# Two of four column groups of a graph-convolution product by Strassen's scheme

## The reference

```
h   = relu(layernorm(x))                 # x: 8 x 2048 x 128, float32
HW  = h @ W                              # W: 128 x 128
A   = relu((adj + adj.T) / 2)            # 2048 x 2048
D   = sum(A, axis=1);  d = D ** -0.5
L   = I - d[:, None] * A * d[None, :]
out = x + relu(L @ HW)                   # for each of the 8 batches
```

## Time and profile before

| what | value |
|---|---|
| time, median of 3 runs | 430.36 us (428.66 to 430.53) |
| the profiled execution | 428.56 us, its span 426.8 us |
| busy: PE, DVE, ACT, POOL | 394.8, 192.5, 115.0, 181.1 us |
| mean granted TensorE clock | 0.991 |
| matmuls of 512 columns in the main phase | 1536 by the code |
| DMA | 42.39 MB, mean 99 GB/s |

### The profile page before, as it was taken

How to read it: one execution, slowest core, us unless ns; L and a number is a source line. 1 busy time by engine, 2 the same in 40 slices (tenths; PEclk the granted TensorE clock), 3 DMA queues, 4 the chain that set the end, 5 groups by cost and what they waited for, 6 DMA issues and landing times.

```text
span 426.8 us, 5828 instructions
## 1 busy us (share of the span) xinstructions
PE 394.8 (93%) x2193; PEld 208.4 (49%) x2193; DVE 192.5 (45%) x519; ACT 115.0 (27%) x235; POOL 181.1 (42%) x295
## 2 busy tenths in 40 slices
PE   4648678999999999999999999999999999999994
PEld 3548653444444444454545454545454545454541
DVE  2697999979789844144614142431010202010211
ACT  1565986665657420102120102110100001010100
POOL 0088702077599957264955445813020111212211
PEclk9987999999999999999999999999999999999999
DMA  8999995103203343030022020031102020203011
GB/s 271 354 372 384 387 281 152 48 0 96 78 2 111 94 117 98 2 92 9 25 75 74 26 74 25 2 98 42 58 27 73 26 74 26 74 10 90 27 49 49
DMA packets 59820, 42.39 MB, mean 99 GB/s; under 512 B 2320, under 2 KB 51600, under 8 KB 59792
## 3 DMA queue, kind: packets, MB, share of 16 engines
q1 hardware_dynamic: 59792, 42.02, 31.8%
HBM read 33.62 MB, written 8.39 MB: 98 GB/s over the span
## 4 chain that ended last, share of the span: by engine, by line
PE 50%; issue 30%; POOL 7%; SPq 4%; DMA 3%; DVE 2%; ACT 2%; POOLq 0%
PE ps L572 14%; PE ps L573 14%; PE ps L574 14%; POOL sums L286 4%; DMA S<-in_adj_dram 3%; SPq L180 3%; PE ps L522 3%; PE ps L536 2%; POOL dsv L277 1%; SPq L195 1%; ACT S L316 1%; PE ps L586 1%; PE ps L587 1%; PE ps L588 1%; POOL xn L268 1%
## 5 line engine op out<-in xcount | busy, mean ns | idle before, releaser
L573 PE MATMUL ps<-S,hbuf 128*128 128x512 f16 x512 | 194.0, 379 | 0.0
L572 PE MATMUL ps<-S,hbuf 128*128 128x512 f16 x496 | 188.0, 379 | 0.0
L574 PE MATMUL ps<-S,hbuf 128*128 128x512 f16 x496 | 188.0, 379 | 0.0
L286 POOL TENSOR_TENSOR sums<-res,sums 128x512 f32<-128x512 f32 x32 | 42.8, 1343 | 160.9 <-DVE res L420 160.9
L573 PEld LDWEIGHTS ps<-S,hbuf 128*128 128x128 f16 x512 | 50.1, 98 | 56.5
L574 PEld LDWEIGHTS ps<-S,hbuf 128*128 128x128 f16 x496 | 48.5, 98 | 58.5
L572 PEld LDWEIGHTS ps<-S,hbuf 128*128 128x128 f16 x496 | 48.5, 98 | 54.9
L412 DVE SCALAR_TENSOR_TENSOR g<-ps,g 128x512 f16<-128x512 f32 x32 | 21.6, 686 | 114.5 <-ACT g L342 114.5
L342 ACT ACTIVATE g<-ps 128x512 f16<-128x512 f32 x32 | 19.0, 593 | 192.0 <-PE ps L574 191.5
L420 DVE SCALAR_TENSOR_TENSOR res<-ps,dsv 128x512 f32<-128x512 f32 x32 | 22.1, 689 | 75.8 <-PE ps L588 75.8
L336 ACT ACTIVATE S<-S,dneg 128x512 f16<-128x512 f32 x62 | 43.5, 719 | 21.6 <-DVE S L407 19.6
(11 more groups left out here) (69 smaller groups left out, 285.0 us busy)
## 6 DMA issues: line engine op xcount, KB each, us to landing
S<-in_adj_dram SPq DMA_DIRECT2D x16, 1024.0 KB, 12.4
hbuf<-in_x_dram SPq DMA_DIRECT2D x64, 128.0 KB, 3.5
sums<-in_x_dram SPq DMA_DIRECT2D x32, 256.0 KB, 2.8
out_dram<-sums SPq DMA_DIRECT2D x32, 256.0 KB, 2.6
res<-in_L_gnn_W_dram SPq DMA_DIRECT2D x1, 64.0 KB, 1.8
```

The costliest lines, as they stand in the source:

```text
L286: nc.gpsimd.tensor_tensor(sums[:, e % SUMS, :], res[:, e % 2, :], sums[:, e % SUMS, :], ALU.add).then_inc(sum_ready, 1)
L572: nc.tensor.matmul(acc, h_hi, l_hi(t), start=(mt == 0), stop=False)
L573: nc.tensor.matmul(acc, h_hi, l_lo(t), start=False, stop=False)
L574: last = nc.tensor.matmul(acc, h_lo, l_hi(t), start=False, stop=(mt == T - 1))
```

## The change

Groups 0 and 1 are computed as before, now as 8 stages of the four quarters (128 slots). Groups 2 and 3 are computed as one 2 x 2 block product for each quarter: A is the two batches by the two halves of the contraction, B the two halves of the contraction by the two column groups. Instead of eight half products there are seven parts P1 to P7 (Winograd's form of Strassen's scheme), in the order P1, P2, P6, P3, P5, P7, P4, each of 8 steps by 3 matmuls of 512 columns. They are four quarters by seven parts after the 128 slots.

- **Operands of B.** Four forms T1 to T4 are sums of blocks of L. For each of 8 rows of blocks, from slot 33 on every 10 slots, ACT scales one block, DVE makes four forms, ACT and DVE split them. T3 stays in S. The other three are written by ACT's own transfers to a DRAM array `t_forms` (48 transfers of 128 KB) and read back by SP to where L's groups 0 and 1 were, after their last use (6 MB each way).
- **Operands of A.** S1 to S4 are made of the halves of h: `join_pair` on POOL (1024 columns), `combine_pair` on DVE (four instructions of 256 columns), `split_pair_hi` on ACT and `split_pair_lo` on DVE (two instructions of 512 columns each), four pairs to a quarter.
- **Results.** P1 is copied out of PSUM by ACT; seven sums on DVE for each quarter give the four tiles, which then go through the same steps as every tile.
- **Normalisation.** With two groups to a quarter in the plain stages, quarter 1 is due at slot 32, quarter 2 at 64, quarter 3 at 96. The power on POOL gives way to a square root on ACT and a reciprocal on DVE (all but the first eight units). For quarters 2 and 3 the eight 128-column instructions go from POOL to ACT and `split_h_lo` from DVE to POOL. A unit now holds tiles u and u+8 in place of 2u and 2u+1, so stage 0 needs unit u at slot u.
- **Other.** The tables of row scales are made 4 times, not 16. Two buffers for x and results (`sums`) in place of three, one for `xn` in place of two. Products with W come at slots 5 and 7 of a stage, not 3 and 5. The last stage's order by batches goes.

```
+G_SCALE = 2.0 ** -16
...
 SPARES = 2
 LEAD = 6
...
+ADD_AT = (8, 10)
...
+CHAIN_HI = (4, 5, 6, 7)
+CHAIN_LO = (5, 6, 7, 8)
+PAIR_AT = (4, 5, 6)
...
+W_PART_AT = ((3, 1), (6, 0), (6, 7))
...
-SUMS = 3
+XN = 1
...
+    PLAIN = QUARTERS * G // 2
+    SLOTS = T * PLAIN
+    PLAIN_TILES = PLAIN * PAIR
+    TILES = 2 * PLAIN_TILES
...
+    ORDER = [1, 2, 6, 3, 5, 7, 4]
...
-    h_slot += [16 + 6 * k for k in range(UNITS)] + [68 + 6 * k for k in range(2 * UNITS)]
-    stat_slot += [h_slot[UNITS + k - k % LN_BATCH] - 8 + k % LN_BATCH for k in range(3 * UNITS)]
+    h_slot += [16, 18, 20, 22, 24, 26, 28, 30]
+    h_slot += [T * 2 + 1 + 4 * k for k in range(UNITS)] + [T * 4 + 1 + 4 * k for k in range(UNITS)]
...
+    form_slot = [33 + 10 * i for i in range(HALF)]
...
+            sp.wait_ge(acc_done, PLAIN_TILES - PAIR)
+            reload_form(1)
+            sp.wait_ge(acc_done, PLAIN_TILES)
+            reload_form(0)
+            reload_form(2)
...
+                if first >= 2 * UNITS:
+                    nc.gpsimd.tensor_tensor(neg_mean, neg_mean, y, ALU.mult).then_inc(rstd_ready, 1)
...
+            def split_h_lo(u):
+                pool.wait_ge(h_hi_ready, u + 1)
+                nc.gpsimd.tensor_tensor(hbuf[:, u, 1, :], xn_buf(u), hbuf[:, u, 0, :], ALU.subtract).then_inc(h_lo2_ready, 1)
...
+                nc.gpsimd.tensor_tensor(pair_buf(n), hbuf[:, u:u + 2, 0, :], hbuf[:, u:u + 2, 1, :], ALU.add).then_inc(pair_ready, 1)
...
...
+                    last = nc.scalar.activation(xn_buf(u, b, b + 1), x_buf(u, b, b + 1), ACT.Relu,
+                                                bias=neg_mean[:, c:c + 1], scale=y[:, c:c + 1])
...
+            def scale_b12(i):
+                b12 = s_piece(chain_of("T3", i))
+                nc.scalar.activation(b12, b12, ACT.Copy, scale=dneg[:, i:i + 1]).then_inc(b12_ready, 1)
...
+            def spill_form(n):
...
+                act.dma_start(t_forms[n % 3, 0, n // 3], form16[:, (n - 1) % FORM_SLOTS, WIDE:2 * WIDE]).then_inc(t_out[n % 3], 16)
+                act.dma_start(t_forms[n % 3, 1, n // 3], form16[:, n % FORM_SLOTS, 0:WIDE]).then_inc(t_out[n % 3], 16)
...
+                act.wait_ge(part_done, len(ORDER) * q + 1)
...
+                nc.scalar.activation(p1_v, two(q, 1), ACT.Copy).then_inc(p1_copied, 1)
...
+            def first_form(i):
...
+                n = 3 * i
...
...
+                    dve.wait_ge(t_out[2], 32 * (i - 1))
+                nc.vector.scalar_tensor_tensor(form[:, n % FORM_SLOTS, :], s_piece(chain_of("B11", i)), npos[:, i:i + 1],
+                                               s_piece(chain_of("T3", i)), ALU.mult, ALU.add).then_inc(t1_ready, 1)
...
+            def split_t_lo(n):
+                dve.wait_ge(t_hi_ready, n + 1)
+                nc.vector.tensor_tensor(form16[:, n % FORM_SLOTS, 0:WIDE], form[:, n % FORM_SLOTS, :],
+                                        form16[:, (n - 1) % FORM_SLOTS, WIDE:2 * WIDE], ALU.subtract).then_inc(t_lo_ready, 1)
...
+            def sum_c11(q):
+                dve.wait_ge(p1_copied, q + 1)
+                dve.wait_ge(part_done, part_at(q, 2) + 1)
+                nc.vector.tensor_tensor(two(q, 2), two(q, 2), p1_v, ALU.add).then_inc(c11_ready, 1)
...
+                dve.wait_ge(v_ready, q + 1)
+                nc.vector.tensor_tensor(two(q, 3), two(q, 3), p1_v, ALU.add).then_inc(c12_ready, 1)
...
+                dve.wait_ge(u_ready, q + 1)
+                nc.vector.tensor_tensor(two(q, 7), two(q, 7), p1_v, ALU.add).then_inc(c22_ready, 1)
...
+            def sum_c21(q):
+                dve.wait_ge(part_done, len(ORDER) * (q + 1))
+                dve.wait_ge(u_ready, q + 1)
+                nc.vector.tensor_tensor(two(q, 4), two(q, 4), w_16, ALU.add).then_inc(c21_ready, 1)
...
+                    nc.vector.tensor_scalar(npos[:], dneg[:], -1.0, None, ALU.mult).then_inc(d_ready, 1)
...
+                    if form_slot[i] + 2 == tau:
+                        if i == 0:
+                            dve.wait_ge(d_ready, 3)
+                        first_form(i)
+                        third_form(i)
+                        second_form(i)
+                        fourth_form(i)
...
+                    sum_c12(q)
+                if k == 6:
...
+                if pair_in(r) is not None:
+                    combine_pair(pair_in(r))
+                if k in SUM_AT:
+                    split_g_lo(e + SUM_AT.index(k))
...
+            take_product(TILES - 2)
+            sum_c21(QUARTERS - 1)
+            split_g_lo(TILES - 1)
+            take_product(TILES - 1)
...
+                nc.tensor.matmul(acc, a_hi, b_hi, start=starts, stop=False)
+                nc.tensor.matmul(acc, a_hi, b_lo, start=False, stop=False)
+                last = nc.tensor.matmul(acc, a_lo, b_hi, start=False, stop=ends)
...
+                    if s % 2 == 0 and mt < UNITS:
+                        u = s // 2 * UNITS + mt
+                        pe.wait_ge(h_lo_ready if u < 2 * UNITS else h_lo2_ready, u % (2 * UNITS) + 1)
+                    products(s, mt)
...
+            for r in range(PARTS):
+                q, k = r // len(ORDER), r % len(ORDER)
+                e = PLAIN_TILES + 4 * q
+                wait_part(q, ORDER[k])
+                for i in range(HALF):
+                    if ORDER[k] in (3, 5, 6, 7) and i % 2 == 0:
+                        pe.wait_ge(s_lo_ready, UNITS // 2 * q + i // 2 + 1)
+                    part(q, ORDER[k], i)
+                    if r == 0 and i in W_AT:
+                        multiply_w(e - 2 + W_AT.index(i))
+                    if q and (k, i) == (0, 6):
+                        multiply_w(e - 1)
+                    if (k, i) in W_PART_AT:
+                        multiply_w(e + W_PART_AT.index((k, i)))
             multiply_w(TILES - 1)
```

## The result

| | before | after |
|---|---|---|
| time, median | 430.05 us (428.66 to 430.53, 4 runs) | 436.30 us (435.38 to 439.62, 4 runs) |
| span of the profiled execution | 426.8 us | 433.7 us |
| mean granted TensorE clock | 0.991 | 0.968 |

The ratio is 1.0165, with a 95% interval of 1.0105 to 1.0225: the kernel became 1 to 2% slower, where 3% faster was forecast.

A forecast was written before the change was run, and what follows sets the result against it. PE was taken as the bound, matmul count times 0.2158 us: 428.56 - 20.7 + 1.3 + 1 + 1.7 + 4.8 = 416.7, stated as a median of 417.3 us. Forecast 412 to 421 (chance 0.50), range 409.5 to 428.5.

The forecast's parts named there:

- Matmuls: PE's main phase: 1440 wide matmuls for 1536, 96 fewer at 0.2158 us each, -20.7 us.
- Stages 0 and 1: DVE's list ahead of L's piece 31: added statistics and splits leave no slack, +1 us (0 to 3).
- Stage 2: Quarter 1's pairs of units on POOL make tile 2's halves for W late, +1.7 us (0 to 4).
- Stages 3 to 5: Forms on ACT and DVE, with POOL collisions and ACT-DVE ping-pong, exceed the stage time: +4.8 us (0 to 13).
- the lock in full: Rival, stages 3 to 5: POOL's and DVE's work in series, 13 us, 424.9 total; chance 0.18 including mixtures up to 428.
- Slots 80 to 128: After statistics and forms end, ACT and DVE catch up; quarter 0's pairs ready by slot 124: 0 us (0 to 2).
- The parts: P1 to P7 of each quarter: tightest W has 1.8 us to spare, so 0 us (0 to 3).
- 2 MB for T2 start in stage 7: SP's queue: T2's reading back starts in stage 7, due 10.4 us after the parts begin; counted as hidden.
- Hidden: SP's queue: reading forms back costs nothing; stores queue behind, but x for tile 16 is wanted only in P3.
- The clock: PE's clock: waits of 1 to 2 us leave PE mostly busy, 0 us (0 to 2, if one is longer).
- The end: After the last wide matmul: DVE's extra take and sum delay ACT, less W's product moved ahead, +1.3 us (0.7 to 3).
- The slower one: Rival, forms: a group runs as one chain, 20.3 us not 13.8, total 444; chance 0.15, of which 0.11 slower.

The follow-up runs named there:

- x0: The kernel before with 96 wide matmuls left out (part of the product missing), nothing else changed: 408.23 us, ratio 0.952.
- x1: The changed kernel with eight slots for the statistics' means and variances in place of four: 435.53 us, ratio 1.015.
- x2: The changed kernel with quarter 0's fourth pair prepared behind the halves of tiles 14 and 15: 437.91 us, ratio 1.021.
- x10: The changed kernel with eight statistics slots, fourth pair later, SP's order mended, and the last sum and halves ahead of take_product(30): 426.96 us, ratio 0.995.
- x14: The changed kernel with only the stages' products with W moved to slots 9 and 11 (addition and store later too): 437.98 us, ratio 1.019.
- x12: x10 with the stages' products with W at slots 9 and 11, not 5 and 7 (addition and store later too): 418.49 us, ratio 0.975.
- x9: The changed kernel with the fourth pair behind tiles 14 and 15 and SP's order of reads and stores mended: 429.64 us, ratio 1.000.
- x15: x12 with join_pair on DVE instead of POOL: 416.73 us, ratio 0.970.
- x6: The changed kernel with split_h_lo of quarters 2 and 3 back on DVE, not POOL: 445.46 us, ratio 1.036.
- x4: The changed kernel with the 48 transfers of forms to DRAM issued by SP in place of ACT: 439.60 us, ratio 1.023.
- x13: x12 with quarter 3's units of h four slots later: 424.81 us, ratio 0.990.
- x3: The changed kernel with join_pair on DVE instead of POOL: 434.51 us, ratio 1.013.

## Why the prediction was wrong

- **Matmuls, -20.7:** right. x0 gave 20.9.
- **Stages 0 and 1, +1:** the step that failed first in time. I counted DVE's load, and not the wait in `statistics` for POOL. The gaps are 7.9 us; without that wait 3.3 remain (x1), against my 1 (0 to 3).
- **Stage 2, +1.7:** 1.1 in the changed kernel, where stage 1 is late by itself; 2.7 in x1.
- **Stages 3 to 5, +4.8:** 5.2 in gaps and 1.3 at half clock, right in size; whether for the reason given no run shows, so it may be luck in part. Its prices hold in part: DVE's instructions with two inputs in SBUF took 0.74 to 1.09 us by group, not 0.67, and ACT's 128-column instructions 0.48 each with 1.65 for four, not 1.1:

```profile
L591 ACT ACTIVATE xn<-hbuf,lnt 128x128 f32<-128x128 f32 x64 | 26.2, 481 | 6.9 <-issue 3.0 <-POOL lnt L481 2.2 <-DVE form L813 1.0
...
L813 DVE TENSOR_TENSOR form<-form 128x512 f16<-128x512 f32 x24 | 20.3, 848 | 4.4 <-ACT form L624 4.4
...
L788 DVE SCALAR_TENSOR_TENSOR S<-S,dneg 128x512 f32<-128x512 f32 x8 | 8.7, 1086 | 0.3
...
L798 DVE SCALAR_TENSOR_TENSOR form<-S,dneg,form 128x512 f32<-128x512 f32 x8 | 6.0, 744 | 0.0
```

A group's mean hides two kinds. The timelines of DVE and POOL, the same line beside POOL's addition of 512 columns (L508) and beside none of that length:

```profile
189.47 1.64 DVE L788 SCALAR_TENSOR_TENSOR S<-S,dneg 128x512 f32<-128x512 f32 x1
...
202.69 0.75 DVE L788 SCALAR_TENSOR_TENSOR S<-S,dneg 128x512 f32<-128x512 f32 x1
...
188.84 1.71 POOL L508 TENSOR_TENSOR sums<-res,sums 128x512 f32<-128x512 f32 x1
```

Of the eight L788 three took 1.64, each ending 0.55 after POOL's L508, and five 0.75. In stages 3 to 5 fourteen of DVE's instructions took over 0.2 longer than the shortest of their kind, 10.4 us together; I had put 4 us a stage. By the rule of the Trainium skill that the prediction cites (SBUF — State Buffer, section Who interferes with whom) such a DVE instruction is locked out by a GpSimd instruction that reads SBUF. The rows of DVE above and L821's 2.06 agree; beside POOL's instructions of 8 columns, which read SBUF too, none was stretched by 0.1 or more, while some of POOL's own took 0.65 where others took 0.20 (L472). The 13 us that I worked out for the lock in full were not paid in PE's gaps.
- **Slots 80 to 128, "ACT and DVE catch up", 0:** the largest error, 5.0 in gap and 3.1 at half clock. The pairs were put at "ready by slot 124", without a sum; but the first join waits for the last form to land (9.3 us of POOL's waiting, start 238.0), each pair takes 7.4 us for the 3.9 of three slots, and the halves of tiles 14 and 15 stand behind the fourth pair. Moving that pair took the gap to 1.2 (x2).
- **The parts, 0 (0 to 3):** 2.9, at the edge of the range. The steps on the queues failed: "2 MB for T2 start in stage 7", but its first transfer was issued at 260.4, after the wait for tile 13's sum, and "Hidden" for x of tile 16 cost POOL 11.4. The steady quarters have 0.6 each, where I gave them 1.8 to spare.
- **The clock, 0 (0 to 2):** 4.4 in all, behind waits of 3.4 and 4.8 where I had 1 to 2. That 1 to 2 us are harmless and longer waits are not is no rule either: see the last section.
- **The end, +1.3:** right, also step by step: from the last wide matmul's start to the last product with W it is 3.8 us for 1.8, 2.0 later as worked out. The two steps are on the rows of DVE and ACT, and the edit in x10 took 1.3 off:

```profile
425.30 0.69 DVE L883 SCALAR_TENSOR_TENSOR res<-ps,dsv 128x512 f32<-128x512 f32 x1 [3.14 <-PE ps L1130]
425.90 0.69 DVE L870 TENSOR_TENSOR ps<-ps,xn 128x512 f32<-128x512 f32 x1
...
426.63 0.60 ACT L660 ACTIVATE g<-ps 128x512 f16<-128x512 f32 x1 [5.79 <-DVE ps L870]
```

**The rivals.** The slower one, a group of forms in series (17.1 us or more), is not what happened: ACT's first instruction of a group (L614) starts at 127.2 in the first and 225.0 in the eighth, 14.0 us apart on average. The loss came, but not by the road to which I had given 0.11. The sign turned by several places of 1.3 to 8 us each, of which my sum had a third: 8.8 us foreseen for 27.8. And they pass each other on. From the start of stage 0 the first join comes after 171.3 us in the changed kernel, after 168.1 in x14 and 165.9 in x12, while PE begins the parts after 191.2, 183.3 and 178.7 (x12's own base, x10: 169.1 and 189.1): with W late the pairs come sooner by less than half of what PE gains. So in the changed kernel the early waits cost little by themselves: taking 4.6 us of gaps away gave 0.8 (x1), taking W's away nothing (x14). The gain came from the late places first: 6.7 us from the fourth pair and SP's order (x9), then 2.7 from the statistics and the end (x10), 8.5 from W's slack (x12) and 1.8 from the joins (x15). That is 13.4 of the 20.7 against the kernel before (430.13 to 416.73).

Not settled: why ACT's and DVE's lists need until 236 us for the forms. DVE is busy 65.4 of the 72.7 us of stages 3 to 5, and x6 shows that more load on it makes them later; x4 speaks against ACT's issues; no run took load from DVE there.

## What to carry to other kernels

Before adding work to in-order lists under a full PE, list for each handover what stands ahead of it on every queue, SP's too, and each semaphore that a moved instruction waits on, not only its length. Begin the repair of such a chain of waits at its last one, and measure two edits together before dropping either, since one cause removed alone may show nothing. Where only a handover is late, first give it slack: moving the products with W by four slots was worth 8.5 us once the rest was in order, and nothing before. The same runs warn that slack at one place exposes the next: with W late, units of h four slots later cost 6.3 us (x13).

## What the runs showed of the hardware

- The length of a single gap in dense work did not tell whether the clock fell to half (1.2 GHz): one of 3.57 us in the changed kernel was followed by 3.4 us at 0.50, one of 3.63 in x9 and one of 3.80 in x12 by none, one of 2.30 in x1 by 3.4 us again; 4.96 brought 6.8 us, 8.9 brought 10.2 (x14).
- A DVE addition of 128 x 256 with both inputs in SBUF took 0.42 us alone, 1.33 to 2.33 when it met POOL's of 1024 columns, and 1.37 beside POOL's addition of 512 columns (the changed kernel).
- A DVE instruction of 128 x 512 with two inputs in SBUF took 0.75 us alone and beside POOL's 8-column instructions, 1.64 when POOL's addition of 512 columns ran (the changed kernel, L788).
- A store of 256 KB issued behind 6 MB of loads on SP's queue landed after 9.4 us; the median of these stores is 2.3 (the changed kernel).
- POOL's addition of 1024 float16 columns took 2.2 us (the changed kernel), DVE's 1.2 (x3).
- An issue of 128 KB took 0.33 and 0.46 us on ACT's queue (the changed kernel), 0.32 and 0.43 on SP's (x4).
